# A decoder layer's self-attention: denominators partly by accumulating DMA, weighted values in pairs of key chunks

## What is computed

```python
qkv = (x @ w_qkv.T).reshape(b, s, 3, H, hd)          # H = 16, hd = 32
scores = jnp.einsum('bhid,bhjd->bhij', q, k) * scale
exp_s = jnp.exp(scores - block_max[..., None])
out = einsum('bhij,bhjd->bhid', exp_s, v) / exp_s.sum(axis=-1)   # written by blocks with a running lse
return attn @ w_out.T
```

## Time and profile before

| what | value |
|---|---|
| runs | 3505.8, 3497.93, 3503.73 us, median 3503.73 |
| profiled execution, its own time | 3506.53 us |
| its span | 3504.4 us |
| PE busy over the span | 3152.3 us, 90% |
| DVE, ACT, POOL busy | 2221.6, 1609.8, 1784.0 us |
| ps_s score matmuls, ps_st matmuls | 2048 and 2048 |
| ps_pv matmul records | 4096 |
| ps_d records with ones on probs (L559) | 1280 |
| POOL adds (L504) | 320, mean 4.58 us |

### The profile page before, as it was taken

How to read it: one execution, slowest core, us unless ns; L and a number is a source line. 1 busy time by engine, 2 the same in 40 slices (tenths; PEclk the granted TensorE clock), 3 DMA queues, 4 the chain that set the end, 5 groups by cost and what they waited for, 6 DMA issues and landing times. The chain is left out here.

```text
span 3504.4 us, 50814 instructions
## 1 busy us (share of the span) xinstructions
PE 3152.3 (90%) x16278; PEld 1803.4 (51%) x16278; DVE 2221.6 (63%) x4046; ACT 1609.8 (46%) x2933; POOL 1784.0 (51%) x605
## 2 busy tenths in 40 slices
PE   7997999999999999999999998696499994888578
PEld 6875444444444444444444443575255553666433
DVE  4334787777777777777877873463366663666423
ACT  2221466666666656666666666221045451222211
POOL 0001587878788778878787878000200002444255
PEclk9997899999999999999999999798699996999679
DMA  4546202112103020030211000597544444432531
GB/s 178 183 156 189 49 16 47 38 25 61 25 17 69 22 65 21 18 70 16 52 34 25 13 7 4 183 263 178 147 111 123 122 125 144 148 145 108 202 95 34
DMA packets 176929, 309.06 MB, mean 88 GB/s; under 512 B 30571, under 2 KB 58155, under 8 KB 173485
## 3 DMA queue, kind: packets, MB, share of 16 engines
q1 hardware_dynamic: 171014, 295.73, 29.2%
q0 software_dynamic: 5696, 10.52, 1.0%
HBM read 187.47 MB, written 126.04 MB: 89 GB/s over the span
## 5 line engine op out<-in xcount | busy, mean ns | idle before, releaser
L617 DVE TENSOR_REDUCE part_max<-ps_s 128x1 f32<-128x512 f32 x2048 | 1268.7, 680 | 310.0 <-PE ps_s L523 310.0
L504 POOL TENSOR_TENSOR added<-added,probs 128x2048 f32<-128x2048 f32 x288 | 1319.9, 4583 | 87.5 <-ACT probs L708 60.6
L708 ACT ACTIVATE probs<-ps_st 128x512 f32<-128x512 f32 x2048 | 1083.3, 600 | 584.1 <-PE ps_st L542 574.4
L542 PE MATMUL ps_st<-q_stack,k_stack 98*128 98x512 f32 x2048 | 861.2, 426 | 11.9 <-ACT probs L708 6.0
L523 PE MATMUL ps_s<-k_stack,q_stack 96*128 96x512 f32 x2048 | 837.8, 425 | 26.1 <-POOL max_parts L493 20.6
L542 PEld LDWEIGHTS ps_st<-q_stack,k_stack 98*128 98x128 f32 x2048 | 387.4, 190 | 517.5 <-ACT probs L708 316.8
L553 PE MATMUL ps_pv<-probs,v_sb 128*32 128x512 f32 x4096 | 548.1, 607 | 0.0
L523 PEld LDWEIGHTS ps_s<-k_stack,q_stack 96*128 96x128 f32 x2048 | 396.2, 194 | 194.6 <-DVE part_max L617 119.9
L504 POOL TENSOR_TENSOR added<-probs 128x2048 f32<-128x2048 f32 x32 | 146.5, 4579 | 303.6 <-ACT probs L708 303.6
L642 DVE RECIPROCAL ps_d<-ps_d 128x128 f32<-128x128 f32 x128 | 121.3, 952 | 109.6 <-PE ps_d L566 103.0
L1585 POOL MEMSET e_bias_rows<- 128x1024 f32 x1 | 1.0, 953 | 369.9 <-POOLq L46 369.9
(11 more groups left out here) (268 smaller groups left out, 3648.6 us busy)
## 6 DMA issues: line engine op xcount, KB each, us to landing
xq_stack<-q_parts SPq DMA_DIRECT2D x66, 384.0 KB
q_stack<-q_hi SPq DMA_DIRECT2D x64, 256.0 KB
k_stack<-k_hi SPq DMA_DIRECT2D x64, 256.0 KB
q_parts<-q_h_out SPq DMA_DIRECT2D x64, 256.0 KB, 4.9
x_in<-in_x_rows SPq DMA_DIRECT2D x8, 1024.0 KB
q_hi<-qk_h_out SPq DMA_DIRECT2D x8, 1024.0 KB
q_lo<-qk_l_out SPq DMA_DIRECT2D x8, 1024.0 KB, 6.4
k_hi<-qk_h_out SPq DMA_DIRECT2D x8, 1024.0 KB, 4.3
```

What stands on the lines that cost most here:

```text
L504: pool.tensor_tensor(added[:, w % 2], left, probs[:, k % RING], ALU.add).then_inc(added_up, 1)
L542: pe.matmul(ps_st[:, n % BANKS], k_stack[:, w // BPB, j, k * P:(k + 1) * P], q_stack[:, w % 4, j], start=True, stop=True).then_inc(item_do ...
L617: dve.tensor_reduce(part_max[:, s:s + 1], ps_s[:, (w * SLOTS + s) % BANKS], AX.X, ALU.max)\
L708: act.activation(probs[:, k % RING, j], ps_st[:, n % BANKS], ACT.Exp, scale=SCALE).then_inc(item_used, 1)
```

## The change

The changed kernel computes the same layer. In self-attention:

- `ADDED` is now 0, 4, 5, 9 to 15: nine POOL adds a unit. Chunks 1, 2, 3 and 6, 7, 8 form two chains: POOL issues a DMA that adds ring slot k - 1 onto slot k in SBUF (`link`), after TensorE has used chunk k for the weighted values. The last slot of a chain then goes through ones as a chain total at chunk 8 (chain 0) and 13 (chain 1). The direct groups go.
- `weighted_values` is called for k - 1 and k together at odd k, and not at even k.
- `added_totals` of a unit moves from its own end to step 4 of the next unit (`LATE`), and the inversions and the normalization from slots 8 to 11 to slots 29 to 32 (`FREED`).
- `SLOTS_AT` changes from 3, 2, 3, 4, 4, 4, 4, 4, ... to 4, 4, 4, 4, 4, 2, 2, 4, ...; the rest stays.
- ScalarE's exponentials wait, beside the adds, for the chain links that read or write their ring slot and for the chain total.
- The hardware loops over turns are written out on all five engines.

```diff
--- before.py
+++ after.py
...
     EARLY = 8
-    SLOTS_AT = [3, 2, 3, 4, 4, 4, 4, 4, 5, 5, 5, 5, 4, 4, 0, 0]
+    SLOTS_AT = [4, 4, 4, 4, 4, 2, 2, 4, 5, 5, 5, 5, 4, 4, 0, 0]
     BANKS = 3
...
     SCALE = float(HD) ** -0.5
-    ADDED = [0, 1, 2, 4, 5, 7, 8, 10, 11, 12, 13]
-    DIRECT = [k for k in range(KT) if k not in ADDED]
+    ADDED = [0, 4, 5, 9, 10, 11, 12, 13, 14, 15]
+    CHAINS = [(1, 2, 3), (6, 7, 8)]
+    TOTALS_AT = {8: 0, 13: 1}
+    LATE = 4
     ADDS = len(ADDED) - 1
...
         pv_done, dens_done, added_up = sem("pv_done"), sem("dens_done"), sem("added_up")
+        chain_summed = [sem(f"chain_summed{c}") for c in range(2)]
         raw_done, inverted, normalized = sem("raw_done"), sem("inverted"), sem("normalized")
...
+        def unit_before(i, w):
+            return (i, w - 1) if w else (i - 1, UPB - 1)
...
         SLOTS_OF = list(slots_of())
+        FREED = SLOTS_OF[LATE + 1][1]
...
                 load_v(1, 1)
-                with sp.Fori(0, TURNS - 1) as i:
+                for i in range(TURNS - 1):
                     body(i, False)
...
+                def add(i, w, n):
+                    k = ADDED[n + 1]
+                    if n == 0 and not (isinstance(i, int) and i == 0 and w < 2):
+                        pool.wait_ge(dens_done, at(i, w, 1, -1))
+                    pool.wait_ge(item_used, items(i, w, item(i, w, k, HEADS - 1) + 1))
+                    if n:
+                        pool.wait_ge(added_up, at(i, w, ADDS, n))
+                    left = added[:, w % 2] if n else probs[:, ADDED[0] % RING]
+                    pool.tensor_tensor(added[:, w % 2], left, probs[:, k % RING], ALU.add).then_inc(added_up, 1)
+                def link(i, w, c, n):
+                    k = CHAINS[c][n + 1]
+                    pool.wait_ge(pv_done, at(i, w, KT, k + 1))
+                    if n:
+                        pool.wait_ge(chain_summed[c], at(i, w, 32, 16 * n))
+                    pool.dma_start(probs[:, k % RING].rearrange("p j q -> p (j q)"),
+                                   probs[:, (k - 1) % RING].rearrange("p j q -> p (j q)"),
+                                   accum_op=ALU.add).then_inc(chain_summed[c], 16)
...
                     for w in range(UPB):
-                        for n, k in enumerate(ADDED[1:]):
-                            if n == 0 and not (isinstance(i, int) and i == 0 and w < 2):
-                                pool.wait_ge(dens_done, at(i, w, 1, -1))
-                            pool.wait_ge(item_used, items(i, w, item(i, w, k, HEADS - 1) + 1))
-                            if n:
-                                pool.wait_ge(added_up, at(i, w, ADDS, n))
-                            left = added[:, w % 2] if n else probs[:, ADDED[0] % RING]
-                            pool.tensor_tensor(added[:, w % 2], left, probs[:, k % RING], ALU.add).then_inc(added_up, 1)
+                        link(i, w, 0, 0)
+                        add(i, w, 0)
+                        add(i, w, 1)
+                        link(i, w, 0, 1)
+                        link(i, w, 1, 0)
+                        add(i, w, 2)
+                        link(i, w, 1, 1)
+                        for n in range(3, ADDS):
+                            add(i, w, n)
                 body(0)
-                with pool.Fori(1, TURNS - 1) as i:
+                for i in range(1, TURNS - 1):
                     body(i)
...
                                        probs[:, k % RING, j], start=(k == 0), stop=(k == KT - 1))
-                    if k in DIRECT:
-                        if k == DIRECT[0] and not begins(i, w):
+                    if k in TOTALS_AT:
+                        c = TOTALS_AT[k]
+                        if c == 0 and not begins(i, w):
                             pe.wait_ge(normalized, at(i, w, 1, 0))
+                        pe.wait_ge(chain_summed[c], at(i, w, 32, 32))
                         for j in range(HEADS):
-                            mm = pe.matmul(ps_d[j * HD:(j + 1) * HD], ones[:], probs[:, k % RING, j],
-                                           start=(k == DIRECT[0]), stop=False)
+                            mm = pe.matmul(ps_d[j * HD:(j + 1) * HD], ones[:], probs[:, CHAINS[c][-1] % RING, j],
+                                           start=(c == 0), stop=False)
                     mm.then_inc(pv_done, 1)
...
                                 turn_max(at(*one, 2, pair + 1), n % BANKS, items(i, w, n - BANKS + 1), pair)
-                            weighted_values(i, w, k)
-                        added_totals(i, w)
+                            if k % 2:
+                                weighted_values(i, w, k - 1)
+                                weighted_values(i, w, k)
+                            if k == LATE and not begins(i, w):
+                                added_totals(*unit_before(i, w))
+                    if last:
+                        added_totals(i, UPB - 1)
...
                 body(0, False)
-                with pe.Fori(1, TURNS - 1) as i:
+                for i in range(1, TURNS - 1):
                     body(i, False)
...
                         two = after(*one)
-                        ended = (i, w - 1) if w else (i - 1, UPB - 1)
+                        ended = unit_before(i, w)
                         if exists(*one):
                             for s in range(EARLY, SLOTS):
-                                if not begins(i, w) and s < EARLY + TPB:
-                                    invert(*ended, s - EARLY)
+                                if not begins(i, w) and FREED <= s < FREED + TPB:
+                                    invert(*ended, s - FREED)
                                 slot_max(*one, s)
-                                if not begins(i, w) and s == EARLY + TPB - 1:
+                                if not begins(i, w) and s == FREED + TPB - 1:
                                     normalize(*ended)
...
                 body(0, False)
-                with dve.Fori(1, TURNS - 1) as i:
+                for i in range(1, TURNS - 1):
                     body(i, False)
...
                         old = k - RING
-                        if old % KT >= ADDED[0]:
-                            before = at(i, w, ADDS, adds_by(old) if old >= 0 else adds_by(KT + old) - ADDS)
-                            act.wait_ge(added_up, before)
+                        if old % KT in ADDED:
+                            act.wait_ge(added_up, at(i, w, ADDS, adds_by(old) if old >= 0 else adds_by(KT + old) - ADDS))
+                        for c, chain in enumerate(CHAINS):
+                            if old % KT in chain[:-1]:
+                                links = chain.index(old % KT) + 1
+                                act.wait_ge(chain_summed[c], at(i, w, 32, 16 * links - (0 if old >= 0 else 32)))
+                            if old % KT == chain[-1]:
+                                done = next(t for t, n in TOTALS_AT.items() if n == c)
+                                act.wait_ge(pv_done, at(i, w, KT, done + 1 - (0 if old >= 0 else KT)))
                     for j in range(HEADS):
...
                 body(0, False)
-                with act.Fori(1, TURNS - 1) as i:
+                for i in range(1, TURNS - 1):
                     body(i, False)
...
```

## The result

The changed kernel takes 3591.4 us (median of four runs, 3587.1 to 3598.7) against 3502.3 for the kernel before beside it: ratio 1.026, 95% interval 1.023 to 1.028, slower by 89 us. The forecast was 3550, its range 3490 to 3615. The profiled execution took 3587.1 us, its span is 3585.2. All of the difference lies in self-attention: the last add ends at 2267.6 instead of 2184.9, +82.7; later stages are as they were within 2 us.

What follows compares the result with a forecast made beforehand. TensorE was taken to set the pace, VectorE a fifth behind. 4.9 us saved a unit become 6.5 of new waits: first unit -1.9, units 1 to 29 +35.0, end +13.0, so 3503.7 + 46 = 3550, range 3490 to 3615.

Steps and rivals of the forecast that it cites:

- Pairs: Weighted values of two chunks together: score matmuls wait for VectorE's reductions; eight slots take 6.28 us, ten 7.50.
- steps 5 to 7: VectorE's inversions, normalization and first maxima delay the S of slot 35: 11.33 us, against 9.0 for TensorE alone.
- The rival in which TensorE stays the bound: VectorE keeps up within pairs and copies are covered: units of 51.3 us, 3351 in all; chance 0.17.
- TensorE's busy share in the stage: Sign in self-attention: TensorE's busy share was to fall to about 86%.
- the two rules that I took: Changing tiling mode drains TensorE, so halving visits pays; tiling speeds TensorE but not the emptying of PSUM.
- Steps 14 and 15: Step 15 waits for ScalarE's copies of the second maxima, no longer hidden: 7.88 us for both steps, against 6.05.
- the forecast's own 3525 to 3580: Range of the main forecast alone, 0.8 us a unit either way, with chance 0.62.
- Link 2: Exponential 10 overwrites its source; 9.0 us from issue to landing allowed, 7 taken, so hidden.
- The late-link rival: Exponential 10 waits for link 2; each us beyond 9.0 costs one in 31 units, 3612 to 3705; chance 0.14.
- Loops: Written out in self-attention, they lose the back edge's gap: 10.6 us saved once.
- Ends: First unit -1.9 us; last two units +13.0, with POOL's six adds ending the stage.

Runs made afterwards that it cites:

- e2: The changed kernel with weighted_values called for each chunk alone again, all else of the change kept: 3480.0 us, ratio 0.9943.
- e11: The kernel before with its loops written out (e1), plus weighted values of two chunks together at odd steps: 3610.9 us, ratio 1.032.
- e3: The changed kernel with each row-maximum reduction reading 256 of 512 columns and the exponential's scale an eighth: 3473.6 us.
- e4: The changed kernel without its four accumulating DMAs a unit and the waits on them, the exponential's scale an eighth: 3570.1 us.
- e9: e2 with key and value loads issued only when the next unit's weighted values 0 to 10 are done: 3456.5 us.
- e5: The changed kernel with the second maxima transposed at step 13, behind its visit, instead of at step 14: 3544.5 us.
- e12: e9 with, in the last unit, chunks 12 to 15 through ones on TensorE instead of four POOL adds: 3448.9 us.
- e1: The kernel before with only its hardware loops in self-attention written out: 3488.8 us, ratio 0.9967.
- e10: The changed kernel with the same move of the key and value loads as e9: 3579.7 us.

## Why the prediction was right, and where it fell short

**Pairs: right, to 0.14 us a step.** Measured against forecast: 6.19 for 6.28, 3.05 for 3.08 (step 4), 11.22 for 11.33 (steps 5 to 7, stall 1.41), 8.24 for 8.38, 7.39 for 7.50, 7.04 for 7.16. The unit without a disturbance is 57.2, forecast 57.9: the differences all have one sign and sum to 0.7, some 0.3 of it because reductions in an unbroken row take 0.607 where I used 0.617. That the pairs are the cause is shown three ways: taken out -111 (e2), put in alone +122 (e11), and the reductions halved brings their steps to TensorE's own time (e3). The -111 and +122 hold the clock drops that come with the pairs. The rival in which TensorE stays the bound fell at the place that it named: waits are 57.2 - 49.9 = 7.3 us a unit, and it needed less than 6.4. One sign did not come as I wrote it: TensorE's busy share in the stage is 94%, not 86, since stalls of a few tenths between pipelined matmuls hardly show in its busy time. Of the two rules that I took from TensorEngine Tiling (Array Packing) in the Trainium skill, Key Properties and PSUM Bottleneck, the second decides here: with single visits, which enter and leave the tiled mode twice as often, a unit takes 54.8 instead of 57.2.

**Steps 14 and 15: the wait right, its consequence missed.** T waits 1.56 for the copies in every unit, and the two steps take 7.87, as forecast. What the sum lacked is that the granted clock can fall after it. It stays up in 9 of 29 units; a fall costs 1.5 us in most and 3.2 where a whole visit is caught. The 29 units take 1709 us where the forecast had 1678.5; undisturbed they would be 29 x 57.2 = 1659. So 50 us are disturbances, against which the base came out 20 shorter than forecast. Three late units, 2.8 to 3.7 us above their neighbours of 58.7, are 9 of the 50; some 40 remain, and they need no link: without any (e4) the 29 units are 43 us over 29 x 57.2.

That the stall sets off the drop, and not the work before it, rests on order in the trace (each drop in the 29 units comes behind a stall of TensorE, of 1.56 for the copies in most, of 1.41 at slot 35 or of 1.1 to 2.0 behind a late link in the others), on e2, where the only drops in the whole units come behind late totals, and on e9, where regular stalls of 0.66 at most go with a clock of 1.00. Against a simple rule stand the 9 units with the same stalls and no drop, and e5. No run held the stall and filled it with other work, so this stays short of proof, and what decides whether the clock falls stays open.

Of the 41 us by which 3550 is short, 30 are here (50 less the 20 of the shorter base) and 6 in the ends; the rest lies between the profiled executions and the medians. That 3591 is still within the range of 3490 to 3615 is in part luck: it lies outside the forecast's own 3525 to 3580, in the stretch that I had given to a late link, and it got there by the clock.

**Link 2: right in size, its issue missed.** The links land in 7.1 us (median; taken 7) from their issue, the least in 6.8. The estimate worked out from two pages of the Trainium skill, Collectives: The Full Stack (section The bandwidth ceiling) and DMA: Bandwidth & Descriptors (section Anatomy of one DMA — SWDGE (gpsimd) path), was 6.8; the trace agrees. The issue holds POOL 0.88. Link 2 itself never takes more than 9.1, where I allowed 9.0; ScalarE waits for it in 17 of the 29 units, but TensorE stalls over 0.5 us behind that in three alone. The late-link rival named the loads as its cause, and these three units are of that kind, but by a path that I had not seen: it is link 1, issued beside the key loads, that takes 10.8, 10.8 and 12.1, and POOL, which waits for it, issues link 2 1.1, 1.1 and 2.4 us behind time. Link 2 then takes 8.8, 8.8 and 8.4. This should have been a term of the sum, not only a rival, since the loads are certain.

**Loops: right**, -12 for -10.6. **Ends:** the stage grew by 82.7, the 29 units by 1709 - 1643.5 = 65.5; the ends take 17, where -1.9 + 13.0 = 11 was forecast. In the last unit TensorE waits 12.3 for POOL's six adds, which e12 removes.

**What the change would have been worth.** Loops -12 (e1), all else but the pairs (chains, late totals and inversions, slots; no run takes these apart) -32 once loads keep clear of links 1 to 3 (e9 against e1), pairs +111 to +122. One unit of e9 is 1.35 under before.

## What to carry to other kernels

Before merging two short interruptions of a matmul stream into a long one, ask who empties its PSUM banks: the consumer idles for the whole merged visit, and with three banks it never gets that time back. Here 2.6 us a unit of entering and leaving saved turned into 5 us of waits (57.2 against 54.8 a unit), and stalls long enough for the clock to fall behind them. And when a chain of transfers has a deadline within a period, put every other large transfer into the part of the period in which no transfer with a near deadline is under way (in e9 the loads overlap link 4, which has time to spare); moving it by eye may hit a worse place.

## What the runs showed of the hardware

- An accumulating DMA of 1 MB from SBUF onto SBUF lands 6.8 us after its issue at best and 7.1 in the median. Beside loads of 256 KB and 1 MB, which themselves take 11 to 13 and 20.5 us, it took 8.9 to 12.1 (link 1 in the changed kernel) and 12.4 to 13.8 (in e2).
- TensorE's granted clock fell for some microseconds behind a single stall of 1.1 to 2 us (0.8 in e5 and e10), in 20 of 29 units and not each time: matmuls of 0.40 lasted 0.63. In e9, with regular stalls under 0.7 us, it was 1.00.
- A Fori back edge cost 10.6 to 12 us once, with all five engines in the loop. Part of it is the clock: behind a gap of 4.6 us TensorE's granted clock was 0.51 over the 14 us from 1284.
